# A product-keys stage with its key splits on GpSimd and its thresholds read from PSUM, and a last mixture-of-experts stage without its hardware loop

## The chip, the core and the metric

The kernel runs on one core of one Trainium2 chip. The metric is the device time of the whole kernel in microseconds (us); the time before is the median of three runs. The core's engines are TensorE (PE; its weight loads are listed as PEld), VectorE (DVE), ScalarE (ACT), GpSimd (POOL) and SyncE (SP, which issues most DMAs). A matmul goes to PSUM, which has eight banks of 512 f32 values a partition; GpSimd can't read PSUM.

## What is computed

Eight layers run one after the other over x of 4 x 1024 tokens of 128 values: four attention-like and four feed-forward, each followed by a layernorm of x plus its result. Two feed-forward layers are touched by the change. The first is the product-keys layer (`L2_ffn`):

```python
xn = _rmsnorm(x, norm_w)
q = (xn @ w_q.T).reshape(b, t, H, 2, DK)          # H = 8 heads
sim1 = einsum('bthd,hkd->bthk', q[..., 0, :], keys[:, :, 0, :])   # 32 keys a side
sim2 = einsum('bthd,hkd->bthk', q[..., 1, :], keys[:, :, 1, :])
s1, i1 = top_k(sim1, 8); s2, i2 = top_k(sim2, 8)
all_sc = s1[..., :, None] + s2[..., None, :]
fs, pk = top_k(all_sc, 8)                          # best 8 of 1024 sums a head
hidden = gelu(einsum('btd,bthkd->bthk', xn, expert_down[fi])) * relu(fs)
return einsum('bthk,bthkd->btd', hidden, expert_up[fi])
```

The second is the last layer (`L3_ffn`): a sigmoid gate picks 2 of 8 experts a token; the token times its score goes through that expert (128 -> 176, squared relu, -> 128, in bf16), and a shared expert in f32 is added.

## The kernel before, in words

Each layer is a stage with programs of its own for the engines, which are tied together by semaphores only. A stage works on batches of 1024 tokens (8 tiles of 128 tokens; a half is 4 tiles). Each engine carries out its program in the order in which it is written, so the order of the calls in the loops is the schedule.

**Product keys** (`product_keys_stage`), 32 tiles of 8 heads. The kernel doesn't gather experts. For each tile and head it makes all 1024 sums of the two sides' scores, keeps those that reach the head's eighth best, and adds the kept levels of all heads to one weight for each of the 1024 experts; that times the gelu of all experts goes through `up`.

- `score` (PE) makes a tile's 512 similarities in one bank of the ring A. `take_sims` (ACT, L1965 and L1966) copies them out in f32 and in bf16. `rest_of` (L2055) and `low_of` (L2061), both on DVE, with `take_middle` (ACT, L1971) between them, split each value in three bf16 parts. `transpose_parts` (PE, L2192) turns these in four fills of the ring, and `take_partsT` (ACT, L1977) copies each fill out. All that is done for tile t + 2 while tile t is at work.
- `build_sum` (PE, L2216) makes the 1024 sums of one head in two banks of the ring S (three banks), two heads ahead. `take_sum` (ACT, L1996) copies the two halves to SBUF, where there is room for four heads.
- `keep` (DVE, L2088) compares a head's sums with its least kept value and multiplies: both inputs are the copy in SBUF.
- `add_level` (PE, L2224) adds eight transposes of the level into the two banks of `weights`. After head 7, `weigh` (DVE, L2095) multiplies `weights` by the gelu; the next tile's `add_level` of head 0 has to wait for that, since it starts the two banks anew.
- `project_down` (PE, L2200) and `gelus` (ACT, L1985) make the gelu of a later half, two fills of A a tile, `project_up` (PE, L2235) is the product with `up`; `finish` and `normalise` (DVE, with GpSimd's `rsqrt` between them) end a half.

Ring A is the queue that all of score, gelu product and turned parts go through, in the order of `fills_of_A`. Before, it has two banks: PE may claim a bank once the fill before the last one has been copied out.

```python
to_act = [m.psum(f"to_act{i}", [P, HALF]) for i in range(2)]
sum_banks = [m.psum(f"sum{i}", [P, HALF]) for i in range(3)]
```

**The last stage** (`routed_experts_stage`) runs a hardware loop over the 4 batches. In a pass PE turns x, makes the gates and the shared expert's hidden values, and turns the scores' parts; then 8 units follow (a pair of experts on one half): `widen` (PE, L3022) spreads the scores, `scale` (DVE, L2926) multiplies x by them, `project_up` (PE, L3032 and L3036), relu (ACT, L2899), `square` (DVE, L2933) and `project_down` (PE, L3049), which has the hidden values as weights and is cut in four matmuls of 128 columns. DVE then adds x and normalises the half. `Fori` passes don't overlap: DVE ends a batch (`finish(1)`, `normalise(1)`) before it begins the gates of the next one. GpSimd squares the shared expert's hidden values (L2866).

## Time and profile before

| | |
|---|---|
| median of 3 runs | 2315.13 us (2308.87 to 2318.24) |
| profiled execution, its own time | 2313.05 us |
| its span, first to last instruction | 2311.2 us |
| product-keys stage | about 930 to 1563 us of the span |
| last stage | about 2136 to 2311 us |
| PE, DVE, ACT, POOL busy over the span | 84%, 69%, 52%, 27% |
| TensorE's granted clock, mean | 0.90 of full speed |

A row of the profile gives a line of the kernel, an engine, what is written from what, the count, and then busy time and mean duration, or (in the timeline) start and duration in us; an x4 in the timeline merges four instructions, and the duration is that of all. "[0.86 <-ACT ...]" is idle time of the engine before the row, and what ended it. Matmuls are pipelined: a group's last one runs on while the next group starts. A row of windows gives the stretch, its length, the busy time (and instructions) of PE, PEld, DVE, ACT and POOL in it, then PEclk, the DMA engines' share and GB/s. PEclk is the granted clock as a share of 2.4 GHz; 0.50 is the lower level, 1.2 GHz.

### The profile page before, as it was taken

To read this page: it belongs to the slowest core of one execution; us is meant where nothing else is said; L and a number is where in the kernel's file an instruction comes from. 1 tells how busy PE (TensorE), PEld (TensorE's weight loads), DVE (VectorE), ACT (ScalarE), POOL (GpSimd) and SP (SyncE) were. 2 spreads that over 40 slices of the span, in tenths; PEclk is the share of its full clock that TensorE was granted. 3 is DMA by queue.
4 is the path that set the end of the run, shared out by engine and by line. 5 is a ranking of instruction groups with operands and counts; after the bars stand their busy time and mean duration, and the time that the engine had idled before them with its cause. 6 is when DMAs were issued, how large, how long until landed. Compare 5 with 4: busy or idle time off the path is not lost. (4 is left out here: it accounts for less than half of the span.)

```text
span 2311.2 us, 33205 instructions
## 1 busy us (share of the span) xinstructions
PE 1950.1 (84%) x10882; PEld 1310.8 (57%) x10882; DVE 1595.5 (69%) x3840; ACT 1203.7 (52%) x2540; POOL 630.5 (27%) x774
## 2 busy tenths in 40 slices
PE   8999789996799995799999999987778776775897
PEld 5666544443577773587778777774324333334544
DVE  4555457785278887388898899873368666676676
ACT  3333355652355542588788877850245444554343
POOL 2222147776012122000000000000055555554111
PEclk9999989997899997799999999996688888887877
DMA  2000010000200000000000000005011111111100
GB/s 83 27 27 18 33 66 1 19 10 10 91 10 10 19 10 5 24 1 6 15 6 3 14 6 6 6 1 198 1 36 38 44 48 47 48 45 56 51 27 27
DMA packets 35266, 68.90 MB, mean 30 GB/s; under 512 B 8598, under 2 KB 19935, under 8 KB 34359
## 3 DMA queue, kind: packets, MB, share of 16 engines
q1 hardware_dynamic: 26934, 50.34, 6.3%
q0 software_dynamic: 8192, 16.79, 2.8%
q8 instruction: 77, 1.26, 0.2%
q14 instruction: 63, 0.51, 0.1%
HBM read 54.52 MB, written 12.58 MB: 29 GB/s over the span
## 5 line engine op out<-in xcount | busy, mean ns | idle before, releaser
L2758 PE MATMUL tk_to_act<-tk_keys,tk_xT 128*128 128x512 f32 x512 | 270.3, 672 | 94.9 <-issue 57.9
L1996 ACT ACTIVATE pk_sums<-pk_sum 128x512 f32<-128x512 f32 x512 | 278.8, 601 | 110.2 <-PE pk_sum L2216 107.8
L2088 DVE SCALAR_TENSOR_TENSOR pk_level<-pk_sums,pk_least 128x1024 f32<-128x1024 f32 x256 | 321.5, 1276 | 7.7 <-ACT pk_sums L1996 6.4
L2442 POOL DMA_INDIRECT tk_values<-top_keys_values,tk_index x256 | 243.9, 953 | 299.0 <-DVE tk_index L2607 224.3
L2224 PE MATMUL pk_weights<-product_keys_early_ident,pk_level 128*128 128x128 f32 x2048 | 271.8, 276 | 31.2 <-DVE pk_level L2088 30.1
L2224 PEld LDWEIGHTS pk_weights<-product_keys_early_ident,pk_level 128*128 128x128 f32 x2048 | 225.5, 141 | 65.1 <-DVE pk_level L2088 49.5
L2507 ACT ACTIVATE tk_scores<-tk_to_act 128x512 f32<-128x512 f32 x256 | 143.3, 594 | 209.7 <-PE tk_to_act L2758 112.3
L2758 PEld LDWEIGHTS tk_to_act<-tk_keys,tk_xT 128*128 128x128 f32 x512 | 101.5, 212 | 243.5 <-issue 181.9
L1667 PEld LDWEIGHTS er_outs<-experts_early_w,er_hT 128*128 128x128 f32 x1024 | 134.0, 192 | 59.8 <-issue 56.4
L1102 PE MATMUL ml_outs<-experts_early_we,ml_xT 128*128 128x512 f32 x320 | 162.5, 635 | 3.0 <-DVE ml_r L967 3.0
L2605 DVE MAX8 tk_best<-tk_scores 128x8 f32<-128x4096 f32 x32 | 141.4, 4418 | 32.1 <-issue 16.3
L2216 PE MATMUL pk_sum<-pk_lay_corners,pk_partsT 96*128 96x256 bf16 x1024 | 154.2, 272 | 4.0 <-DVE pk_weighed L2095 3.1
L2607 DVE FIND_INDEX8 tk_index<-tk_best,tk_scores 128x8 uint32<-128x4096 f32 x32 | 141.4, 4419 | 0.0
L223 POOL TENSOR_TENSOR pk_plus_eps<-pk_moments,pk_eps 128x4 f32<-128x4 f32 x8 | 11.9, 1482 | 466.3 <-DVE pk_moments L207 466.3
L1667 PE MATMUL er_outs<-experts_early_w,er_hT 128*128 128x128 f32 x1024 | 134.5, 275 | 0.0
L1369 ACT ACTIVATE er_hT<-er_to_act,experts_early_b 128x512 f32<-128x512 f32 x128 | 85.6, 687 | 93.1 <-PE er_to_act L1656 92.2
L1656 PE MATMUL er_to_act<-er_xT,experts_early_w 128*128 128x512 f32 x256 | 133.4, 603 | 0.0
L1977 ACT ACTIVATE pk_partsT<-pk_to_act 96x1024 bf16<-96x1024 bf16 x128 | 131.6, 1033 | 0.0
L967 DVE SCALAR_TENSOR_TENSOR ml_r<-ml_outs,ml_gates,ml_r 128x128 f32<-128x128 f32 x384 | 103.3, 341 | 19.7 <-PE ml_outs L1102 15.6
L2216 PEld LDWEIGHTS pk_sum<-pk_lay_corners,pk_partsT 96*128 96x128 bf16 x1024 | 99.2, 97 | 29.9 <-DVE pk_weighed L2095 11.1
L854 ACT ACTIVATE ml_scaled<-ml_outs,ml_gates 128x128 f32<-128x128 f32 x256 | 70.2, 390 | 84.0 <-PE ml_outs L1102 84.0
L1102 PEld LDWEIGHTS ml_outs<-experts_early_we,ml_xT 128*128 128x128 f32 x320 | 59.7, 201 | 63.6 <-issue 50.3
(396 smaller groups left out, 3731.5 us busy)
## 6 DMA issues: line engine op xcount, KB each, us to landing
tk_scores<-top_keys_compress SPq DMA_DIRECT2D x1, 4096.0 KB
tk_values<-top_keys_values,tk_index POOLq DMA_INDIRECT x256
att_x_proj<-x_first SPq DMA_DIRECT2D x4, 512.0 KB, 5.2
att_x_res<-x_first SPq DMA_DIRECT2D x4, 512.0 KB
x_after_attention<-att_y SPq DMA_DIRECT2D x4, 512.0 KB
ml_x<-x_after_attention SPq DMA_DIRECT2D x4, 512.0 KB, 3.4
experts_early_w<-experts_w SPq DMA_DIRECT2D x2, 1024.0 KB
x_after_attention<-ml_y SPq DMA_DIRECT2D x8, 256.0 KB, 2.0
```

The source lines that it names most:

```text
L1102: pe.matmul(outs[f % len(outs)][:], xT[:, b % 2, t * P:(t + 1) * P], we[:, n * PER_FILL:(n + 1) * PER_FILL, :].rearrange("p e d -> p (e d) ...
L1656: pe.matmul(bank[:], w1[:, n, :], xT[:, t % 2, :], start=True, stop=True).then_inc(A.full.sem, 1)
L1667: ins = pe.matmul(bank[:, s * P:(s + 1) * P], hT[:, (t * CHUNKS + n) % (LAG + 1), s * P:(s + 1) * P], w2[:, n, :], start=k == 0 and s == 0 ...
L1996: act.activation(sums[:, n % SUMS, half * HALF:(half + 1) * HALF], bank[:], ACT.Copy).then_inc(S.free.sem, 1)
L2088: dve.scalar_tensor_tensor(level[:, n % LEVELS, :], sums[:, n % SUMS, :], least[:, t % 2, h:h + 1], sums[:, n % SUMS, :], ALU.is_ge, ALU.m ...
L2216: ins = pe.matmul(by_column[:, j], partsT[:, t % 3, h * FILLS + c, :], lay_corners[:, c], start=True, stop=True)
L2224: ins = pe.matmul(weights[:, ch * P:(ch + 1) * P], level[:, n % LEVELS, ch * P:(ch + 1) * P], ident[:], is_transpose=True, start=h == 0 an ...
L2442: pool.indirect_dma_start(out=values[:, slot, k, :], out_offset=None, in_=c["values"], in_offset=bass.IndirectOffsetOnAxis(ap=index[slot][ ...
L2507: act.activation(scores[:, t % KEPT, ch * HALF:(ch + 1) * HALF], bank[:], ACT.Copy).then_inc(S.free.sem, 1)
L2605: steps.link(dve.max(best[:, slot, :], scores[:, t % KEPT, :]))
L2607: dve.max_index(index[slot][:], best[:, slot, :], scores[:, t % KEPT, :]).then_inc(index_ready, 1)
L2758: pe.matmul(bank[:], xT[:, b, at * P:(at + 1) * P], keys[:, ch * HALF:(ch + 1) * HALF], start=True, stop=True).then_inc(S.full.sem, 1)
```

## The change

In the product-keys stage: `rest_of` and `low_of` move from DVE to GpSimd, at a tile's start; `sum_banks` become two tiles of two banks each, so that DVE's `keep` reads one of its inputs in PSUM, and `build_sum` of head n + 2 waits until `keep` of head n is done; `take_sum` is one copy of 1024 values; ring A gives up a bank and has one. `keep` of head 0 comes ahead of `weigh` of the tile before. `project_up` is halved between heads 0 and 1, the gelu products and the part transposes follow the level in each head.

```diff
-    SUMS = 4
+    SUMS = 2
-        to_act = [m.psum(f"to_act{i}", [P, HALF]) for i in range(2)]
-        sum_banks = [m.psum(f"sum{i}", [P, HALF]) for i in range(3)]
+        to_act = [m.psum("to_act", [P, HALF])]
+        sum_banks = [m.psum(f"sum{i}", [P, E]) for i in range(SUMS)]
...
+            def rest_of(t):
+                pool.wait_ge(A.free.sem, taken_from_A("sims", t, 0))
+                pool.tensor_tensor(rest[:], sims[:, t % KEPT, 0:SIMS].rearrange("p (c k) -> p c k", k=KEYS),
+                                   parts[:, :, 0, :], ALU.subtract)
+            def low_of(t):
+                pool.wait_ge(middle_ready, t + 1)
+                pool.tensor_tensor(parts[:, :, 2, :], rest[:], parts[:, :, 1, :], ALU.subtract)
...
+            def take_sum(n):
+                act.wait_ge(sum_full, n + 1)
+                act.activation(sums[:, n % SUMS, :], sum_banks[n % SUMS][:], ACT.Copy).then_inc(sum_kept, 1)
...
-                    take_sum(next_built(t * HEADS + h))
+                    if t * HEADS + h + SUMS < UNITS:
+                        take_sum(t * HEADS + h + SUMS)
+                    gelus(beside[h:h + 1])
+                    if chained and h == 1:
+                        take_middle(t + 2)
...
-                dve.scalar_tensor_tensor(level[:, n % LEVELS, :], sums[:, n % SUMS, :], least[:, t % 2, h:h + 1],
+                dve.scalar_tensor_tensor(level[:, n % LEVELS, :], sum_banks[n % SUMS][:], least[:, t % 2, h:h + 1],
                                          sums[:, n % SUMS, :], ALU.is_ge, ALU.mult)
...
                 for h in range(HEADS):
+                    keep(t, h)
                     if h == 0 and t > 0:
                         weigh(t - 1)
-                    keep(t, h)
...
+            def build_sum(n):
                 t, h = divmod(n, HEADS)
                 pe.wait_ge(A.free.sem, taken_from_A("partsT", t, FILLS - 1))
+                after(pe, level_ready, n - SUMS + 1)
...
                     if h == 0:
                         if chained:
                             score(t + 2)
-                        project_down(beside[0:1])
                         after(pe, weighed_ready, t)
-                    build_sum(next_built(t * HEADS + h))
-                    if chained:
-                        if h >= HEADS - FILLS:
-                            transpose_parts(t + 2, h - (HEADS - FILLS))
+                    if t * HEADS + h + SUMS < UNITS:
+                        build_sum(t * HEADS + h + SUMS)
                     add_level(t, h)
-                    if h == 0 and t > 0:
-                        project_up(t - 1)
+                    if h < 2:
+                        if t > 0:
+                            project_up(t - 1, range(h * PER_HALF, (h + 1) * PER_HALF))
+                        project_down(beside[h:h + 1])
+                    if chained and h >= HEADS - FILLS:
+                        transpose_parts(t + 2, h - (HEADS - FILLS))
```

PE where one tile of product keys ends and the next begins (L2192 the parts, L2224 the level, L2182 the score, L2200 a gelu product, L2216 the sums, L2235 the product with up), before:

```order
L2192 MATMUL pk_to_act<-pk_ident_b,pk_parts 96x128 x8
L2224 MATMUL pk_weights<-product_keys_early_ident,pk_level 128x128 x8
L2182 MATMUL pk_to_act<-pk_w_sim,pk_xnT 128x512
L2200 MATMUL pk_to_act<-pk_xnT,product_keys_early_down 128x512
L2216 MATMUL pk_sum<-pk_lay_corners,pk_partsT 128x16x16 x4
L2224 MATMUL pk_weights<-product_keys_early_ident,pk_level 128x128 x8
L2235 MATMUL pk_to_dve<-product_keys_early_up,pk_weighed 128x128 x8
```

and in the change (L2171 the parts, L2161 the score, L2197 the level, L2179 a gelu product, L2189 the sums, L2209 the product with up):

```order
L2197 MATMUL pk_weights<-product_keys_early_ident,pk_level 128x128 x8
L2171 MATMUL pk_to_act<-pk_ident_b,pk_parts 96x128 x8
L2161 MATMUL pk_to_act<-pk_w_sim,pk_xnT 128x512
L2189 MATMUL pk_sum<-pk_lay_corners,pk_partsT 128x16x16 x4
L2197 MATMUL pk_weights<-product_keys_early_ident,pk_level 128x128 x8
L2209 MATMUL pk_to_dve<-product_keys_early_up,pk_weighed 128x128 x4
L2179 MATMUL pk_to_act<-pk_xnT,product_keys_early_down 128x512
```

Two fills of ring A, the last parts and the score, now stand next to each other, where a level stood between them; the gelu product moved behind the level.

ACT over heads 0 to 4 of a tile in the change (L1973 and L1974 the similarities, L1997 the sums, L1993 a gelu, L1979 the middle part, L1985 the turned parts):

```order
L1973 ACTIVATE pk_sims<-pk_to_act 128x512
L1974 ACTIVATE pk_parts<-pk_to_act 128x16x32
L1997 ACTIVATE pk_sums<-pk_sum 128x1024
L1993 ACTIVATE pk_gelu<-pk_to_act 128x512
L1997 ACTIVATE pk_sums<-pk_sum 128x1024
L1993 ACTIVATE pk_gelu<-pk_to_act 128x512
L1979 ACTIVATE pk_parts<-pk_rest 128x16x32
L1997 ACTIVATE pk_sums<-pk_sum 128x1024 x3
L1985 ACTIVATE pk_partsT<-pk_to_act 96x1024
```

The second gelu and the middle part now both stand ahead of the copy of head 4's sums; before, the second gelu came after it.

In the last stage the loop is written out over all 32 units. The next batch's x, gates, shared hidden values and parts are made in units 0 to 5 of the batch before (x in three buffers, the rest in two); a half is finished two units after its last product. `project_down` takes its weights as the stationary side, with one matmul of 512 columns for four of 128; the result is the half turned, so ACT copies it out (`take_out`) and PE turns it back (`turn_out`, four transposes) for DVE. Ring A has two banks instead of three.

```diff
-            with dve.Fori(0, B) as b:
...
+            for unit in range(ALL):
+                b, u = divmod(unit, UNITS)
+                more = b + 1 < B
+                if unit + 1 < ALL:
+                    scale(unit + 1)
+                for k in range(PER_UNIT):
+                    square(unit, k)
+                if u == 2 and b > 0:
+                    finish(b - 1, 1)
+                if u == 3 and b > 0:
+                    normalise(b - 1, 1)
+                if more and u == 3:
+                    score_of(b + 1)
+                if more and u == 4:
+                    parts_of(b + 1)
+                if u == 6:
+                    finish(b, 0)
+                if u == 7:
+                    normalise(b, 0)
...
-                        for i in range(PER_HALF):
-                            last = pair == PAIRS - 1 and k == PER_UNIT - 1 and i == PER_HALF - 1
-                            ins = pe.matmul(out[g][:, i * P:(i + 1) * P], hidden[0:units, n % HIDDEN_SLOTS, i * P:(i + 1) * P],
-                                            w, start=False, stop=last)
+                    ins = pe.matmul(outs[g][:], w, hidden[0:units, n % HIDDEN_SLOTS, :], start=False,
+                                    stop=pair == PAIRS - 1 and k == PER_UNIT - 1)
```

## Rows read from the trace of the kernel before

**Rows 1.** Windows of the product-keys stage and of one of its tiles: busy time by engine

```profile
930.00:1565.00 635.00, 582.48 (x4896) 488.79 (x4896) 534.11 (x1385) 486.74 (x875) 31.95 (x27) 0.98 0.02 8
1003.37:1021.16 17.79, 17.35 (x151) 14.65 (x150) 15.83 (x39) 16.73 (x42) 2.20 (x2) 1.00 0.01 1
```

**Rows 2.** Timeline, product keys, heads 5 to 7 of a tile: start, duration, engine

```profile
1000.52 1.04 PE L2224 MATMUL pk_weights<-product_keys_early_ident,pk_level 128*128 128x128 f32 x8
...
1001.18 1.05 ACT L1977 ACTIVATE pk_partsT<-pk_to_act 96x1024 bf16<-96x1024 bf16 x1
...
1001.40 0.60 PE L2216 MATMUL pk_sum<-pk_lay_corners,pk_partsT 96*128 96x256 bf16 x4
...
1001.84 0.61 PE L2192 MATMUL pk_to_act<-pk_ident_b,pk_parts 128*96 128x128 bf16 x8
1002.08 1.12 ACT L1996 ACTIVATE pk_sums<-pk_sum 128x512 f32<-128x512 f32 x2
...
1002.29 1.04 PE L2224 MATMUL pk_weights<-product_keys_early_ident,pk_level 128*128 128x128 f32 x8
```

**Rows 3.** Timeline, product keys, the start of the next tile

```profile
1003.17 1.02 PE L2182 MATMUL pk_to_act<-pk_w_sim,pk_xnT 128*128 128x512 f32 x2
1003.37 1.23 DVE L2095 TENSOR_TENSOR pk_weighed<-pk_weights,pk_gelu 128x1024 f32<-128x1024 f32 x1 [1.47 <-PE pk_weights L2224]
...
1004.22 0.30 PEld L2200 LDWEIGHTS pk_to_act<-pk_xnT,product_keys_early_down 128*128 128x128 f32 x2 [0.86 <-ACT pk_partsT L1977]
...
1006.77 1.95 PE L2235 MATMUL pk_to_dve<-product_keys_early_up,pk_weighed 128*128 128x128 f32 x16
...
1008.56 0.60 PE L2216 MATMUL pk_sum<-pk_lay_corners,pk_partsT 96*128 96x256 bf16 x4
```

**Rows 4.** Groups by line: the thresholds

```profile
L2088 DVE SCALAR_TENSOR_TENSOR pk_level<-pk_sums,pk_least 128x1024 f32<-128x1024 f32 x256 | 321.5, 1276 | 7.7 <-ACT pk_sums L1996 6.4
```

**Rows 5.** Timeline, VectorE: starts of four of the 32 gelu products

```profile
985.58 1.22 DVE L2095 TENSOR_TENSOR pk_weighed<-pk_weights,pk_gelu 128x1024 f32<-128x1024 f32 x1 [1.47 <-PE pk_weights L2224]
...
1040.39 1.23 DVE L2095 TENSOR_TENSOR pk_weighed<-pk_weights,pk_gelu 128x1024 f32<-128x1024 f32 x1 [1.34 <-PE pk_weights L2224]
...
1060.52 1.22 DVE L2095 TENSOR_TENSOR pk_weighed<-pk_weights,pk_gelu 128x1024 f32<-128x1024 f32 x1 [1.34 <-PE pk_weights L2224]
...
1521.79 1.22 DVE L2095 TENSOR_TENSOR pk_weighed<-pk_weights,pk_gelu 128x1024 f32<-128x1024 f32 x1 [1.48 <-PE pk_weights L2224]
```

**Rows 6.** Timeline, ScalarE: the copy of one gelu fill, first tile

```profile
953.48 0.59 ACT L1985 ACTIVATE pk_gelu<-pk_to_act 128x512 f32<-128x512 f32 x1
```

**Rows 7.** One line of the routed-token stage: a GpSimd tensor_tensor of this size

```profile
L1332 POOL TENSOR_TENSOR er_base<-er_y,er_out_b x8: 1265/1266/1272, 644.3 to 891.4; 128x512 f32<-128x512 f32 x8
```

**Rows 8.** Timeline, last stage: VectorE with and TensorE at half clock

```profile
2163.08 1.08 DVE L2933 TENSOR_TENSOR moe_hidden<-moe_relu 128x512 bf16<-128x512 bf16 x3
...
2165.28 1.08 DVE L2933 TENSOR_TENSOR moe_hidden<-moe_relu 128x512 bf16<-128x512 bf16 x3
...
2203.19 1.03 PE L3022 MATMUL moe_scores_wide<-moe_partsT,moe_lay 24*128 24x512 bf16 x2
...
2207.25 1.03 PE L3022 MATMUL moe_scores_wide<-moe_partsT,moe_lay 24*128 24x512 bf16 x2
```

**Rows 9.** Windows, last stage: half clock, then the three gaps between last finishes

```profile
2196.00:2216.00 20.00, 20.00 (x81) 8.89 (x80) 14.20 (x29) 9.46 (x18) 0.00 (x0) 0.50 0.00 0
2179.88:2222.56 42.68, 39.73 (x216) 21.19 (x216) 31.01 (x83) 17.89 (x32) 6.49 (x8) 0.76 0.11 37
2222.56:2261.25 38.69, 34.99 (x216) 19.00 (x216) 28.17 (x84) 17.55 (x32) 6.53 (x8) 0.87 0.13 41
2261.25:2303.14 41.89, 38.23 (x216) 21.09 (x216) 28.36 (x83) 17.67 (x32) 6.53 (x8) 0.80 0.08 25
```

**Rows 10.** Timeline, last stage: a VectorE subtraction beside a GpSimd square

```profile
2148.63 1.04 POOL L2866 TENSOR_TENSOR moe_s_hidden<-moe_s_relu 128x512 f32<-128x512 f32 x1 [12.46 <-ACT moe_s_relu L2889]
2148.81 0.94 DVE L236 TENSOR_TENSOR moe_rest<-moe_score,moe_parts 128x64 f32<-128x64 f32 x1
```

More of the change, by code:

```diff
@@ new lines, in turn_out @@
+            def turn_out(b, g):
+                half = b * HALVES + g
+                pe.wait_ge(outT_ready, half + 1)
+                after(pe, turned_free, half)
+                for i in range(PER_HALF):
+                    ins = pe.transpose(turned[:, i * P:(i + 1) * P], outT[:, g, i * P:(i + 1) * P], ident[:])
+                ins.then_inc(turned_full, 1)
+            for g in range(HALVES):
+                transpose_x(0, g)
+            gates(0)
+            for n in range(SHARED):
+                shared_hidden(0, n)
```

572 lines of the change are left out of this document (300 added, 272 removed).

## The prediction, made before the changed kernel ran

> **What bounds the kernel now.** The change touches two stages, so I read those and leave the rest of the span alone. I took the windows of each stage first, then one ordinary tile of product keys in the timeline, then the waits, and last the batches of the last stage.
>
> In product keys the row of one tile shows PE busy for 17.35 of 17.79 us at the full clock, DVE 15.83, ACT 16.73 [rows 1]: PE sets the pace. What PE's work amounts to comes from start to next start. A level takes 0.88, a head's sums 0.44, a fill of turned parts 0.45 [rows 2]; the last matmul of a group runs on for 0.16 after that (1.04 against 0.88), so the score and each gelu product, 1.02 long, occupy 0.86, and the product with `up` 1.79 [rows 3]. A tile is 8 x (0.88 + 0.44) + 4 x 0.45 + 3 x 0.86 + 1.79 = 16.7 us. PE therefore waits only about 1.1 us a tile: for the last parts' copy and for `weigh` at the tile's start [rows 3], and once for a threshold. The change leaves PE's matmuls in this stage as they are, so that 1.1 us is all that it can win in an ordinary tile. From the first to the thirtieth gelu product there are 29 tiles in 536.2 us [rows 5]; at 17.79 they would be 515.9, so tiles that end a half or start a batch cost 20.3 more (one gap of 20.13 is in [rows 5]).
>
> In the last stage the three gaps between last `finish`es are 42.68, 38.69 and 41.89 us, mean 41.1, with DVE busy 31.0, 28.2 and 28.4 [rows 9]. At full clock a unit takes 2.20 us and DVE paces it; at the lower clock, 1.2 GHz, it takes 4.06 and PE paces it [rows 8]. In 2196 to 2216 the clock is 0.50 throughout [rows 9]. The other 10 to 13 us of a gap are the drain of one pass and the gates of the next, in which DVE and PE take turns.
>
> **Product keys, part by part.** *Splits to GpSimd.* 64 subtractions leave DVE. On GpSimd I price one at 1.27 us, from a tensor_tensor of the same 128x512 f32 [rows 7]. I cost them at nothing: the first starts when the similarities are copied, the second must be done before PE turns the parts at head 4, four heads later, over 8 us of PE's work, and even three times the price fits. DVE's 1.4 us a tile don't shorten the tile either, as DVE isn't the pace.
>
> *Threshold from PSUM.* Not in the trace in this form; the nearest row from below is DVE's 1024-wide product with one input in PSUM, 1.22 us [rows 3], from above the present threshold, 1.28 [rows 4]. I take 1.28. What counts is the new wait: PE builds the sums of head n + 2 only after the threshold of head n. One turn of that circle is 0.44 + 0.16 for the sums, 0.1 hand-over, 1.03 copy (an ACT copy of 1024 takes 1.05 [rows 2]), 0.05, 1.28, 0.06: 3.1 us for two heads. PE's own work for two heads is 2.64 (heads 2, 3) to 3.54 (4 to 7), so the circle binds where heads are light and is nearly tight elsewhere.
>
> *One bank for ring A.* PE can't write a fill before ACT has emptied the one before. In heads 4 to 7 the parts (0.16 to end, 0.1, copy 1.03, 0.05 = 1.34) are hidden by the next head's sums and level (1.32), with ACT's sum copies between them (0.90 from start to start [rows 2]): I carry 0.1 a tile. At the tile's end nothing stands between the last parts and the next score: PE has no other work and waits the whole **1.33 us**. Before, the same place cost part of the 0.86 of [rows 3], because a second bank was free for the score.
>
> *Head 4.* ACT has, after the second gelu product's last matmul: 0.16 + 0.1, gelu 0.50 (0.59 less the usual overlap [rows 6]), middle part 0.50, copy of head 4's sums 1.03, hand-over 0.05, threshold 1.28, 0.06 = 3.7 us, while PE has two heads, 2.64: **1.05 us** of waiting that the old order didn't have in this size.
>
> *Threshold ahead of `weigh`.* It takes the 0.3 to 0.6 us off that PE waits at a tile's start now, but the wait of 1.33 lies over the same time: `weigh` is done before the score is. So nothing is added for it.
>
> An ordinary tile becomes 16.7 + 1.33 + 0.1 + 1.05 = 19.2 us, 1.4 more; over 29 tiles +41. In tiles that end a half, `finish` now falls into head 4's wait, and only `normalise` shows; by the same walk the extras fall from 20.3 to about 13.5: 7 ends of halves at 0.9, three norms of x at 1.7, three turned x at 0.7: -7.
>
> *First tiles.* 8 gelu fills and 8 of parts now alternate between PE and ACT. A gelu fill is 0.86 + 0.16 + 0.1 + 0.59 + 0.05 = 1.76 against 0.9 to 1.0 now (ACT's pace); a parts fill 0.45 + 1.34 = 1.79 against 0.9. That is 16 x 0.85 and two scores, +15; with PE idle half the time its clock may stay at 1.2 GHz, which makes it up to +30. I take +20. *Last two tiles*: no fills, the threshold ahead of `weigh` helps, -2.
>
> Product keys: +41 - 7 + 20 - 2 = **+52 us**. Ends: +12 (head 4's wait absent, first tiles at +13) and +85 (first tiles +30, 0.8 us more a tile where ACT's order holds up heads 5 to 7).
>
> **Last stage.** What is written out lets a batch's gates run beside the one before: a gap falls from 41.1 to DVE's work. I take 28.4 from the undisturbed gaps [rows 9] plus 1.1 for stalls: 29.5, three times -11.6 = -35. The down projection streams as many columns as before (one matmul of 512 for four of 128), so PE stays at 3.84 of the 4.06 at 1.2 GHz and about 1.9 at 2.4 GHz, below DVE's 2.20. The end is longer by the copy of the turned half (0.6), its turning and two hand-overs: +2. The clock is the open part. It fell here after stretches in which PE waited for DVE at a batch's start, and those go away but for one; I leave three half-clock units, 3 x 1.86: +6. **-27 us**, ends -38 (never slow, no stalls) and -3 (half of the 32 units at 4.06: 16 x 1.86 = 30 back, less 2 of gaps).
>
> A row weighs on it: a subtraction of 64 columns took 0.94 us beside a GpSimd square of two SBUF inputs, until that ended [rows 10]; such squares now run in the middle of units. The Trainium skill's "SBUF — State Buffer", section "Who interferes with whom", says that a DVE instruction with two SBUF inputs and a GpSimd instruction that reads SBUF exclude each other, and one with a single SBUF input doesn't; the trace agrees on the first half. By it the new threshold would run freely beside GpSimd's splits, where the old form, held up twice a tile, would have cost DVE up to 2.5 us.
>
> **Sum.** +52 - 27 = +25. Against the profiled execution (2313.05, span 2311.2) that is 2338; the median shown is 2.1 higher, so I give **2340 us**.
>
> **Rivals.**
> *Product keys nearly as fast as before* (ends faster): the head 4 wait vanishes because ACT reaches the fifth sums in time, the waits that remain are 1.33 a tile (18.05 us, +7 over 29), the first tiles cost 13, and the last stage wins 33. +12 - 33 = -21: **2294**. It decides at the ordinary tile: at 20 - 2 - 7 + 29 d = 27 the two stages cancel, d = 0.55, a tile of 18.3 us. For it: ACT is busy 16.73 of 17.79, but loses 0.06 a head with one copy for two, and DVE loses 1.4 us. Against: the order of ACT's program. Chance 0.25.
> *The gains and losses cancel*: waits as walked, but first tiles at the full clock and the last stage at its best, or a tile of 18.3: **2315**. Chance 0.13.
> *Last stage mostly at 1.2 GHz*: PE paces it, -3: **2364**. For it: 20 us on end at 0.50 with PE never idle [rows 9]. Chance 0.09.
> *Product keys lose the clock*: with 2.5 us of waiting a tile PE falls to 1.2 GHz for a part. A tile's 16.7 us of PE become 33.4, 14 more than 19.2; five tiles are +70: **2410**. Now the tile runs at 1.00 throughout [rows 1]. Chance 0.08. The Trainium skill's "TensorE: Matmul & The Clock Gate", Part 4, holds that transposes don't count as activity for the clock. The row speaks against it: 96 of the tile's 151 matmuls are transposes, at clock 1.00; by the page the stage should have run at the lower level already.
>
> **How the numbers follow.** The forecast has 0.45, with a range of its own of 2327 to 2362. No change means within 0.5% (11.6 us, 2303.5 to 2326.7), about what a measurement of this kernel can tell. Faster 0.25 is the first rival, same 0.13 the second, slower 0.45 + 0.09 + 0.08 = 0.62. The range 2290 to 2375 leaves out the clock rival (0.08) and the far part of the first (0.1).
>
> **What would show it.** In the changed trace: PE idle 1.3 us before each score, released by the copy of the parts; PE waiting about 1 us for a threshold before head 4; gaps between gelu products of 19.2; DVE's threshold at 1.2 to 1.3 us; the first threshold about 20 us later; last finishes 29 to 32 us apart. A gap below 18.3, or a score that starts at once, makes the prediction wrong.

## The result, and the profile after the change

| | before | after |
|---|---|---|
| median of this comparison | 2312.72 us (4 runs) | 2352.91 us (4 runs, 2343.39 to 2353.88) |
| ratio, 95% interval | 1 | 1.016 (1.0128 to 1.0198) |
| profiled execution, its span | 2311.2 us | 2350.2 us |
| first to last gelu product (32 tiles) | 568.5 us | 607.9 us |
| ordinary tile of product keys | 17.79 us | 19.35 us |
| first gelu product at | 985.6 us | 1009.6 us |
| top keys, not touched: last store of product keys to last `y` | 568.1 us | 575.5 us |
| last stage: from there to the end | 181.1 us | 149.3 us |

The kernel got slower by 1.6%. Product keys end 63.4 us later, the last stage is 31.8 us shorter, and the 7.4 us between them lie in a stage that nobody changed. Nine other profiles put that stage at 562 to 585 us with no pattern (three more at 465 to 470, see below), so they are its scatter.

Windows of product keys in the changed kernel, the stage and one tile (columns as in [rows 1]):

```profile
930.00:1628.00 698.00, 589.97 (x4879) 488.23 (x4879) 501.27 (x1321) 468.55 (x617) 92.37 (x88) 0.95 0.02 6
1131.95:1151.27 19.32, 17.25 (x150) 14.56 (x150) 14.65 (x38) 13.98 (x17) 2.25 (x2) 1.00 0.01 2
```

PE is busy 17.25 us, against 17.35 in [rows 1], but the tile is 1.5 longer. DVE has 1.2 us less to do. ACT's 16.73 in [rows 1] is not that of an ordinary tile: eight squares of the next batch are in it, and tiles without them have 14.7, so ACT has 0.7 less. Neither shortens anything. The timeline shows where PE stands still. At a tile's end, then at the light heads of the same tile:

```profile
1130.12 0.62 PE L2171 MATMUL pk_to_act<-pk_ident_b,pk_parts 128*96 128x128 bf16 x8
...
1130.78 1.03 ACT L1985 ACTIVATE pk_partsT<-pk_to_act 96x1024 bf16<-96x1024 bf16 x1
...
1131.95 1.10 PE L2161 MATMUL pk_to_act<-pk_w_sim,pk_xnT 128*128 128x512 f32 x2 [1.21 <-ACT pk_partsT L1985]
...
1139.22 0.60 ACT L1993 ACTIVATE pk_gelu<-pk_to_act 128x512 f32<-128x512 f32 x1 [1.56 <-PE pk_to_act L2179]
...
1139.71 0.62 ACT L1979 ACTIVATE pk_parts<-pk_rest 128x512 bf16<-128x512 f32 x1
1140.23 1.93 ACT L1997 ACTIVATE pk_sums<-pk_sum 128x1024 f32<-128x1024 f32 x2
...
1140.77 1.04 PE L2197 MATMUL pk_weights<-product_keys_early_ident,pk_level 128*128 128x128 f32 x8
1141.28 2.48 DVE L2075 SCALAR_TENSOR_TENSOR pk_level<-pk_sum,pk_least,pk_sums 128x1024 f32<-128x1024 f32 x2 [1.51 <-ACT pk_sums L1997]
1142.71 0.60 PE L2189 MATMUL pk_sum<-pk_lay_corners,pk_partsT 96*128 96x256 bf16 x4 [0.90 <-DVE pk_level L2075]
```

Read it from start to start. The last parts' matmuls begin at 1130.12 and would be followed 0.45 us later; the score begins at 1131.95, so 1.38 us are lost, and ACT's copy of those parts fills them. The level of 1140.77 would be followed at 1141.65, and the sums begin at 1142.71: 1.06 lost. With 0.15 for the parts and 0.07 behind the score that is 2.66 on PE's 16.7, which gives 19.36.

The groups by line say the same for the whole stage: the threshold takes 1278 ns against 1276 in [rows 4], but DVE is idle 158 us ahead of it where it was 7.7, and PE waits for it at the sums:

```profile
L2075 DVE SCALAR_TENSOR_TENSOR pk_level<-pk_sum,pk_least,pk_sums 128x1024 f32<-128x1024 f32 x256 | 324.6, 1278 | 158.3 <-ACT pk_sums L1997 157.8
...
L2189 PE MATMUL pk_sum<-pk_lay_corners,pk_partsT 96*128 96x256 bf16 x1024 | 154.9, 273 | 41.0 <-DVE pk_level L2075 38.6
```

The gelu products on DVE, first, thirtieth and last:

```profile
1009.63 1.22 DVE L2082 TENSOR_TENSOR pk_weighed<-pk_weights,pk_gelu 128x1024 f32<-128x1024 f32 x1
...
1587.77 1.22 DVE L2082 TENSOR_TENSOR pk_weighed<-pk_weights,pk_gelu 128x1024 f32<-128x1024 f32 x1
...
1617.52 1.22 DVE L2082 TENSOR_TENSOR pk_weighed<-pk_weights,pk_gelu 128x1024 f32<-128x1024 f32 x1 [1.19 <-PE pk_weights L2197]
```

From first to thirtieth 578.1 us, 41.9 more than in [rows 5]; from there to the last 29.7 against 32.3. The first is 24.1 late, but that is not the whole price of the start, since in this pair the stage also began 4.4 us earlier in the changed kernel. Its first matmuls, before and then changed:

```profile
930.65 13.81 PE L2163 MATMUL pk_to_dve<-product_keys_early_keys,product_keys_early_wq 128*128 128x16 f32 x64 [8.31 <-PEq L154]
```

```profile
926.22 13.81 PE L2142 MATMUL pk_to_dve<-product_keys_early_keys,product_keys_early_wq 128*128 128x16 f32 x64 [8.24 <-PEq L154]
```

From there the first gelu product took 54.9 us before and 83.4 after: 28.5 more. In the stage's first tiles the windows read, for before and then for the changed kernel:

```profile
964.00:972.00 8.00, 5.93 (x57) 4.33 (x57) 5.47 (x23) 7.81 (x13) 0.00 (x0) 1.00 0.01 3
```

```profile
964.00:972.00 8.00, 4.17 (x18) 2.25 (x18) 0.00 (x0) 3.29 (x5) 0.00 (x0) 0.50 0.00 0
```

The clock column is the point. Before, the clock was at its upper level from about 950; after, it stays at 0.50, which is 1.2 GHz, until 996, and one gelu fill then takes 2.82 us:

```profile
954.56 2.04 PE L2179 MATMUL pk_to_act<-pk_xnT,product_keys_early_down 128*128 128x512 f32 x2 [0.78 <-ACT pk_gelu L1993]
957.38 2.05 PE L2179 MATMUL pk_to_act<-pk_xnT,product_keys_early_down 128*128 128x512 f32 x2 [0.78 <-ACT pk_gelu L1993]
```

In the last stage, the windows up to and between the four `finish`es of second halves (as [rows 9]; the last batch has no next one beside it):

```profile
2235.23:2265.63 30.40, 29.92 (x132) 12.28 (x133) 25.99 (x73) 19.25 (x35) 5.53 (x6) 1.00 0.03 9
2265.63:2296.03 30.40, 29.66 (x127) 12.03 (x130) 29.42 (x84) 18.82 (x34) 7.02 (x8) 1.00 0.11 36
2296.03:2325.87 29.84, 28.58 (x116) 10.72 (x118) 29.31 (x85) 17.64 (x32) 7.03 (x8) 1.00 0.05 18
2325.87:2342.76 16.89, 14.70 (x58) 5.47 (x58) 15.72 (x51) 9.36 (x17) 2.56 (x4) 1.00 0.04 16
```

The first line is only the stretch of the same length ahead of the first of them; the gaps are the other lines, 30.4, 29.8 and 16.9 where [rows 9] had 41.1 on average. So the three gaps together are 46.1 us shorter, while the first batch, which now has the second one's preparation beside it and is finished later, takes 14.9 longer from the stage's start to its `finish`. In the gap of 30.40 DVE is busy for 29.42 and PE for 29.66, so these rows don't tell which of the two sets the pace. The clock stays at 1.00.

### The profile page after: what moved, and what is told of

Same layout as the page of the kernel before. It is cut to its first block and busy times, and to the rows that moved or that the text cites. A ratio compares the mean times of both kernels' runs of the same rounds, so it can differ in the third digit from the quotient of the medians.

```text
span 2350.2 us, 31320 instructions
## 1 busy us (share of the span) xinstructions
PE 1935.5 (82%) x10521; PEld 1277.3 (54%) x10530; DVE 1562.8 (66%) x3776; ACT 1191.0 (51%) x2292; POOL 690.5 (29%) x838
## 5 line engine op out<-in xcount | busy, mean ns | idle before, releaser
L2075 DVE SCALAR_TENSOR_TENSOR pk_level<-pk_sum,pk_least,pk_sums 128x1024 f32<-128x1024 f32 x256 | 324.6, 1278 | 158.3 <-ACT pk_sums L1997 157.8
L1997 ACT ACTIVATE pk_sums<-pk_sum 128x1024 f32<-128x1024 f32 x256 | 258.8, 1021 | 54.0 <-PE pk_sum L2189 53.8
L2197 PE MATMUL pk_weights<-product_keys_early_ident,pk_level 128*128 128x128 f32 x2048 | 266.5, 273 | 0.5 <-DVE pk_level L2075 0.5
L2197 PEld LDWEIGHTS pk_weights<-product_keys_early_ident,pk_level 128*128 128x128 f32 x2048 | 232.3, 141 | 4.1 <-DVE pk_level L2075 0.9
L2189 PE MATMUL pk_sum<-pk_lay_corners,pk_partsT 96*128 96x256 bf16 x1024 | 154.9, 273 | 41.0 <-DVE pk_level L2075 38.6
L1923 POOL TENSOR_TENSOR pk_rest<-pk_sims,pk_parts 128x512 f32<-128x512 f32 x32 | 36.0, 1124 | 406.0 <-ACT pk_parts L1974 406.0
L2189 PEld LDWEIGHTS pk_sum<-pk_lay_corners,pk_partsT 96*128 96x128 bf16 x1024 | 92.3, 97 | 109.0 <-issue 98.8
L1985 ACT ACTIVATE pk_partsT<-pk_to_act 96x1024 bf16<-96x1024 bf16 x128 | 130.9, 1022 | 22.5 <-PE pk_to_act L2171 22.5
L967 DVE SCALAR_TENSOR_TENSOR ml_r<-ml_outs,ml_gates,ml_r 128x128 f32<-128x128 f32 x384 | 103.3, 340 | 16.9 <-PE ml_outs L1102 15.1
```

The lines of the kernel that those rows point to most:

```text
L1997: act.activation(sums[:, n % SUMS, :], sum_banks[n % SUMS][:], ACT.Copy).then_inc(sum_kept, 1)
L2075: dve.scalar_tensor_tensor(level[:, n % LEVELS, :], sum_banks[n % SUMS][:], least[:, t % 2, h:h + 1], sums[:, n % SUMS, :], ALU.is_ge, ALU ...
L2189: ins = pe.matmul(by_corner[:, i, j], partsT[:, t % 3, h * FILLS + c, :], lay_corners[:, c], start=True, stop=True)
L2197: ins = pe.matmul(weights[:, ch * P:(ch + 1) * P], level[:, n % LEVELS, ch * P:(ch + 1) * P], ident[:], is_transpose=True, start=h == 0 an ...
```

## The experiments

The runs form four groups, each with its own runs of before: medians of 2311.4, 2319.8, 2202.8 and 2317.1 us. In the third group the untouched top-keys stage took 465 to 470 us, some 100 less than in all others, so totals compare only within a group, and across groups I compare stages. The totals (median, number of runs, and the median of before in the same group) and the stage lengths of all profiles, in us:

| run | total / before | ordinary tile | first gelu product | from the stage's first matmul | first to last | last stage |
| --- | --- | --- | --- | --- | --- | --- |
| before | 2312.7 (4) | 17.79 | 985.6 | 54.9 | 568.5 | 181.1 |
| after | 2352.9 (4) / 2312.7 | 19.35 | 1009.6 | 83.4 | 607.9 | 149.3 |
| e1_last_stage | 2293.8 (4) / 2311.4 | 17.79 | 986.6 | 55.0 | 568.5 | 156.1 |
| e2_product_keys | 2382.0 (4) / 2311.4 | 19.35 | 1010.1 | 83.4 | 607.9 | 174.1 |
| e3_one_bank | 2419.0 (1) / 2311.4 | 20.1 | 1016.5 | 84.8 | 647.5 | 174.3 |
| e4_banks_back | 2289.9 (4) / 2311.4 | 17.80 | 986.6 | 54.8 | 564.5 | 156.5 |
| e7_middle_later | 2347.1 (1) / 2319.8 | 18.85 | 1014.1 | 83.4 | 602.5 | 151.2 |
| e8_score_later | 2371.1 (1) / 2319.8 | 19.53 | 1014.5 | 86.5 | 615.7 | 149.2 |
| e9_spread | 2317.2 (1) / 2319.8 | 18.77 | 1011.4 | 85.8 | 584.4 | 149.2 |
| e10_prep_serial | 2363.2 (1) / 2319.8 | 19.35 | 1014.2 | 83.4 | 607.9 | 158.7 |
| e11_one_bank_new_order | 2243.1 (1) / 2202.8 | 19.16 | 1009.8 | 84.2 | 601.4 | 151.6 |
| e12_best | 2171.5 (4) / 2202.8 | 17.65 | 982.0 | 55.4 | 560.5 | 151.3 |
| e13_best_dve_splits | 2217.3 (5) / 2202.8 | 18.8 to 20.4 | 982.3 | 55.3 | 602.6 | 151.0 |
| e14_middle_ahead | 2258.9 (6) / 2317.1 | 16.87 | 981.9 | 54.8 | 540.7 | 149.0 |

**Each stage alone.** The edits are whole functions: `routed_experts_stage` of the change in the kernel before, and `product_keys_stage` of the change in the kernel before.

> Product keys of before, last stage of the change. If the two stages are independent, this is before less what the last stage gained in the traces (180.8 us from the last store of top keys to the end before, 149.0 after, 31.8): 2281 us, product keys at 17.79 us a tile as before. Rival: the last stage gained only because it came later or after a differently loaded product-keys stage, or part of the 31.8 is scatter of that stage's clock: then 2290 to 2300, with slow units at clock 0.50 in the last stage.

> Product keys of the change, last stage of before. Product keys' last store came 63.4 us later in the changed kernel: 2376 us, if this is the stage's own cost. Top keys, which the change doesn't touch, took 568.1 us before and 575.5 after (last store to last store); rival: these 7 us belong to the change (what it leaves in flight at the stage's end), then this run shows 575 again, otherwise anything between 568 and 576 is the stage's own scatter.

Measured: 0.990 of before (0.984 to 0.996) and 1.033 (1.028 to 1.038). The tile lengths are those of before and after to 0.02 us, so neither stage changes the other's pace. Product keys alone cost 3.3%, more than the whole change, and the last stage gives part of it back. The total of the first run, 2293.8 us, is not the 2281 that I expected but lies in the range of the rival: part of the 31.8 us is scatter of that stage. The last stage of before scatters as well, 174.1 us in the second run against 181.1, so its gain is 18 to 32 us over these profiles. Top keys took 574.4 and 564.9 us, so its 7 us did not follow the product keys. In the first run the last stage was 156.1 and not 149.3, and the windows show units at the lower clock:

```profile
2168.00:2176.00 8.00, 7.74 (x25) 3.89 (x23) 4.45 (x10) 3.95 (x7) 0.00 (x0) 0.50 0.00 0
2176.00:2184.00 8.00, 8.00 (x23) 4.04 (x23) 3.29 (x8) 1.90 (x4) 0.00 (x0) 0.56 0.01 3
```

The units of the first batch ran at 1.2 GHz for some 20 us here and in e4_banks_back, and not in the changed kernel.

**One bank alone.**

```
-        to_act = [m.psum(f"to_act{i}", [P, HALF]) for i in range(2)]
+        to_act = [m.psum("to_act", [P, HALF])]
```

> Before, with one bank in ring A in place of two, all else as it was, last stage too. If the single bank is what costs the stage's start, the first gelu product comes at 1005 to 1012 us as in the changed kernel (1009.6), against 985.6. A tile has then the wait before the score (about 1.3 us, of which before already had 0.5), and, as in this order the first gelu product follows the score at once, a second one for the copies of the similarities (about 1.3): 19.2 to 20.2 us a tile, product keys 60 to 95 us longer, 2375 to 2405. Rival, the bank costs little and the loss is the new head order and the threshold's circle: a tile stays below 18.3 and the first gelu product below 995.

Measured: 2419.0 us in one run, a tile of 20.1, the first gelu product at 1016.5, product keys 110 us longer. The tile is inside what I gave, the start 4 us, product keys 15 and the total 14 us above it. The second wait is there, behind the score:

```profile
1107.56 1.10 PE L2182 MATMUL pk_to_act<-pk_w_sim,pk_xnT 128*128 128x512 f32 x2 [0.69 <-ACT pk_partsT L1977]
1108.70 0.60 ACT L1965 ACTIVATE pk_sims<-pk_to_act 128x512 f32<-128x512 f32 x1 [1.28 <-PE pk_to_act L2182]
1109.93 1.10 PE L2200 MATMUL pk_to_act<-pk_xnT,product_keys_early_down 128*128 128x512 f32 x2 [1.27 <-ACT pk_parts L1966]
```

So with the old order one bank is dearer than in the change, whose order puts the sums and a level behind the score.

**The banks back.** The changed kernel, with two banks in ring A, three of 512 for the sums and four copies of sums in SBUF:

```
-    SUMS = 2
+    SUMS = 4
+    AHEAD = 2
...
-        to_act = [m.psum("to_act", [P, HALF])]
-        sum_banks = [m.psum(f"sum{i}", [P, E]) for i in range(SUMS)]
+        to_act = [m.psum(f"to_act{i}", [P, HALF]) for i in range(2)]
+        sum_banks = [m.psum(f"sum{i}", [P, HALF]) for i in range(3)]
...
-                dve.scalar_tensor_tensor(level[:, n % LEVELS, :], sum_banks[n % SUMS][:], least[:, t % 2, h:h + 1],
+                dve.scalar_tensor_tensor(level[:, n % LEVELS, :], sums[:, n % SUMS, :], least[:, t % 2, h:h + 1],
```

> The changed kernel with the banks of before: two in ring A, three of 512 for the sums, sums built two heads ahead, and so the threshold from two SBUF copies; the new order, the splits on GpSimd and the new last stage stay. My theory (one bank and the two-deep circle are the loss; order and splits cost nothing): a tile at 16.9 to 17.6 us, the first gelu product at 985, product keys 10 to 25 us below before, 2260 to 2275 in all. Rival 1, GpSimd's splits hold up the threshold with two SBUF inputs: thresholds of 2 us and more beside L1923 and L1929, a tile above 18.5, 2300 or more. Rival 2, the new order itself (second gelu product ahead of the middle part, level before the turned parts) is the loss: a tile of 18.5 to 19.3.

Measured: 0.990 of before (0.985 to 0.995). The start is back at 986.6 and the tile at 17.80: the whole loss goes with the banks, and both rivals fall. But the tile didn't go below 17.79, and the total of 2289.9 us is above the 2260 to 2275 that I expected. PE loses 0.44 us at the tile's start, where it asks for `weigh` before it builds sums that don't need it, and 0.34 and 0.29 at heads 3 and 4, where ACT is late:

```profile
1098.90 0.61 PE L2198 MATMUL pk_sum<-pk_lay_corners,pk_partsT 96*128 96x256 bf16 x4 [0.23 <-DVE pk_weighed L2087]
...
1105.25 0.60 ACT L1995 ACTIVATE pk_gelu<-pk_to_act 128x512 f32<-128x512 f32 x1 [1.49 <-PE pk_to_act L2184]
...
1105.74 0.62 ACT L1981 ACTIVATE pk_parts<-pk_rest 128x512 bf16<-128x512 f32 x1
1106.26 2.05 ACT L2002 ACTIVATE pk_sums<-pk_sum 128x512 f32<-128x512 f32 x4
1106.36 0.38 PE L2198 MATMUL pk_sum<-pk_lay_corners,pk_partsT 96*128 96x256 bf16 x2
...
1106.91 0.39 PE L2198 MATMUL pk_sum<-pk_lay_corners,pk_partsT 96*128 96x256 bf16 x2 [0.16 <-ACT pk_sums L2002]
```

**Bank and circle apart.** The kernel of the last run with one bank in ring A (the edit of e3_one_bank).

> The kernel with the banks of before (17.80 us a tile, first gelu product at 986.6), with one change: ring A has one bank, the other bank lies unused. This parts the two things that the banks back undid together. By my steps the single bank brings the 1.38 us before the score, less the 0.44 that PE there already waited for weigh, and all of the first tiles: a tile at 18.6 to 18.9, the first gelu product at 1009 to 1014. Then the two-deep circle is worth the other 0.5 to 0.8 of 19.35. Rival, the circle is the larger part: a tile of 18.0 to 18.3 here.

Measured: a tile of 19.16 and the first gelu product at 1009.8. The single bank is 1.36 of the 1.55 us a tile and all of the start. The rest of the bank layout (the two-deep circle, and with it the threshold from PSUM and the single copy of 1024) adds only 0.19. The 1.36 is a net figure: 1.44 us before the score and some 0.35 around the parts and behind the score, less the 0.44 for `weigh`, which the bank's wait now covers. My expectation was 0.3 too low: the 0.62 at heads 3 and 4 stays, and each fill of parts waits 0.05 to 0.1.

**The two waits of the changed tile.** On ACT the middle part behind the fifth head's sums:

```
-                    if chained and h == 1:
+                    if chained and h == 2:
                         take_middle(t + 2)
```

> The changed kernel with the middle part's copy moved on ACT from ahead of the fifth head's sums to behind them. My step for head 4 (gelu 0.5, middle 0.5, sums 1.03, threshold 1.28 against two heads of PE): PE's wait before head 4 falls by 0.5 us, a tile from 19.37 to 18.9, product keys 13 to 15 us shorter, the waits before the score unchanged. Rival, the wait comes from the two-deep circle alone and only moves: a tile stays at 19.2 to 19.4.

Measured: a tile of 18.85, as the step says. But first to last is only 5.4 us shorter, not 13 to 15: the four tiles that only end a half grew from 20.91 to 21.6 and 22.42, and the three that also turn the next batch's x stayed at 22.06. Perhaps `finish`, which the wait at head 4 had hidden, came into the open; no run shows it.

The score behind the first level:

```
                     if h == 0:
-                        if chained:
-                            score(t + 2)
                         after(pe, weighed_ready, t)
...
                     add_level(t, h)
+                    if h == 0 and chained:
+                        score(t + 2)
```

> The changed kernel with the score moved on PE from the tile's start to behind the first head's sums and level (and on ACT the similarities behind that head's sums). My step for ring A (1.33 us of waiting before each score, because nothing stands between the last parts and it): that wait is covered and goes; what comes in its place is 0.5 us for weigh, which the wait covered, and 0.3 to 0.6 for the gelu product that now waits for the copies of the similarities: a tile at 18.9 to 19.2, 19.37 in the changed kernel. Rival, PE's time at the tile's start is set by DVE (threshold, weigh) and not by the bank: a tile stays at 19.3 or grows.

Measured: 19.53, the rival's result. The wait for the bank is gone, and these two stand in its place:

```profile
1138.21 0.61 PE L2189 MATMUL pk_sum<-pk_lay_corners,pk_partsT 96*128 96x256 bf16 x4 [0.83 <-DVE pk_weighed L2082]
...
1141.83 1.10 PE L2179 MATMUL pk_to_act<-pk_xnT,product_keys_early_down 128*128 128x512 f32 x2 [0.38 <-ACT pk_parts L1974]
```

From start to start 1.0 and 0.55 us. I had taken the first at 0.5, as if the sums of 0.44 could run beside `weigh`; but PE asks for `weigh` ahead of them.

Both, and the gelu products one head later:

```
                     if h < 2:
                         if t > 0:
                             project_up(t - 1, range(h * PER_HALF, (h + 1) * PER_HALF))
-                        project_down(beside[h:h + 1])
+                    if h in (1, 2):
+                        project_down(beside[h - 1:h])
```

> The changed kernel with both moves, and with the two gelu products behind the levels of heads 1 and 2 in place of 0 and 1. By my steps the score's wait is covered, the gelu products no longer wait for the similarities, and the fifth head's sums come ahead of the second gelu: 16.7 of work, 0.5 for weigh, 0.1 for the parts, up to 0.5 at one of the heads 4 or 5: 17.8 to 18.2 us a tile, product keys 30 to 45 us shorter than in the changed kernel, the first gelu product still at 1009. Rival, the two-deep circle (3.1 us for two heads, 2.64 of PE) holds up each light head and sets the tile: 18.8 or more.

Measured: 18.77, first to last 23.5 us shorter than in the change. Between my two figures, nearer the rival's: `weigh` 1.0, and the circle 0.6 and 0.4 at heads 5 and 6:

```profile
1140.35 0.60 PE L2190 MATMUL pk_sum<-pk_lay_corners,pk_partsT 96*128 96x256 bf16 x4 [0.43 <-DVE pk_level L2076]
...
1142.55 0.60 PE L2190 MATMUL pk_sum<-pk_lay_corners,pk_partsT 96*128 96x256 bf16 x4 [0.28 <-DVE pk_level L2076]
```

No order tried brings the change's banks to the tile of before.

**The last stage without its overlap.** The next batch's preparation in one piece, on PE:

```
+                if more and u == 7:
+                    for g in range(HALVES):
+                        transpose_x(b + 1, g)
+                    gates(b + 1)
+                    for n in range(SHARED):
+                        shared_hidden(b + 1, n)
+                    transpose_parts(b + 1)
                 if unit + 1 < ALL:
                     widen(unit + 1)
```

and the same on ACT and DVE.

> The changed kernel; in its last stage the next batch's turned x, gates, shared hidden units and parts are all made ahead of the eighth unit, in one piece, where the change spreads them over units 0 to 5. The orientation of the down projection, the copies and the third x buffer stay. If the overlap is the gain, the gap of last finishes goes back from 30.0 to 40 to 43 us, the stage costs 30 to 38 more, and the clock falls below 1.00 after a batch's start as it did before: 2385 in all. Rival, the gain is the down projection in one matmul of 512 columns for four of 128 and the clock that it keeps: gaps of 32 to 35.

Measured: gaps of 33.8 and 33.9, the stage 158.7 us against 149.3, the rival's range. PE and DVE do take turns again where the next batch starts, but for a short while:

```profile
2257.37 0.60 PE L3079 MATMUL moe_scores_wide<-moe_partsT,moe_lay 24*128 24x512 bf16 x2 [1.10 <-ACT moe_partsT L2906]
...
2257.89 1.29 DVE L2978 TENSOR_TENSOR moe_scaled<-moe_scores_wide,moe_xT 128x512 bf16<-128x512 f32 x2 [2.56 <-PE moe_scores_wide L3079]
```

Without the spreading the stage is 9 us longer, where the change as a whole took 25 to 32 us off at a steady upper clock. The first part of the expectation holds for the clock alone: it fell to 0.50 in both gaps and once ahead of them, for 3.4 us each time (2250.6 to 2254.0 is the first), so the 9 us hold the price of that too. The rest lies in what this run kept: units that still run across the border of a batch, outputs finished two units later, the down projection in its new orientation, the clock. I didn't part those.

**A version that beats both.** From e4_banks_back, with its own waits edited. First the wait for `weigh` behind the sums and the middle part at head 2; then the same with both splits on DVE:

```
                     if h == 0:
                         if chained:
                             score(t + 2)
-                        after(pe, weighed_ready, t)
                     if t * HEADS + h + AHEAD < UNITS:
                         build_sum(t * HEADS + h + AHEAD)
+                    if h == 0:
+                        after(pe, weighed_ready, t)
```

> The kernel with the banks of before, with the two waits edited that its timeline still shows: PE asks for weigh behind the sums of the tile's first head in place of ahead of them (0.44 us), and ACT copies the middle part behind the sums of the fifth head (0.34 and 0.29 at heads 3 and 4). 17.80 less up to 1.05: a tile at 16.8 to 17.1, extras of ends of halves 0.3 to 1.0 larger because finish comes into the open, product keys 15 to 28 us shorter, 2255 to 2270 in all. Rival, PE isn't the pace any more below 17.8 (DVE 15.27 or ACT 13.1 to 16.7 busy in a tile, or the threshold's chain): a tile stays at 17.5 or more.

> The same as the run before it, with both splits back on DVE (rest behind the threshold of head 1, low behind that of head 3). If the splits on GpSimd are worth nothing, as I costed them, this is the same time within 3 us and a tile within 0.1. DVE is busy 15.27 in a tile of 17.80 without them, 16.6 with them. Rival, at a tile of 16.9 DVE with the splits becomes the pace or delays single thresholds: 0.3 to 0.8 us a tile, 8 to 25 us longer.

Measured: 0.986 of before (0.983 to 0.988) with a tile of 17.65, the rival's; and 1.007 (1.005 to 1.010) with tiles of 18.8 to 20.4. In the first, GpSimd's low part now ran beside thresholds that read two SBUF inputs, and both got longer. The low part begins inside one threshold and takes 0.6 us more than alone, the next threshold begins inside the low part and takes 0.6 more:

```profile
1083.87 1.28 DVE L2080 SCALAR_TENSOR_TENSOR pk_level<-pk_sums,pk_least 128x1024 f32<-128x1024 f32 x1 [0.99 <-ACT pk_sums L2002]
...
1084.43 1.74 POOL L1931 TENSOR_TENSOR pk_parts<-pk_rest,pk_parts 128x512 bf16<-128x512 f32 x1 [5.86 <-ACT pk_parts L1981]
...
1085.36 1.90 DVE L2080 SCALAR_TENSOR_TENSOR pk_level<-pk_sums,pk_least 128x1024 f32<-128x1024 f32 x1 [0.21 <-ACT pk_sums L2002]
```

In the second I had expected the same time within 3 us; it was 46 us longer, beyond the rival's 8 to 25 too. DVE's low part waits for the middle part and holds the thresholds behind it:

```profile
1406.42 0.69 DVE L2047 TENSOR_TENSOR pk_parts<-pk_rest,pk_parts 128x512 bf16<-128x512 f32 x1 [2.20 <-ACT pk_parts L1963]
```

That comes from where ACT makes the middle part here, so the run doesn't tell what the splits on DVE cost in a better order; that wasn't tried.

Last, the middle part ahead of the second gelu, in the 1.49 us that ACT waits for PE there:

```
+                    if chained and h == 1:
+                        take_middle(t + 2)
                     gelus(beside[h:h + 1])
-                    if chained and h == 1:
-                        take_middle(t + 2)
```

> The kernel with the banks of before, PE's wait for weigh behind the first sums, and ACT's middle part ahead of the second gelu, where ACT waits 1.49 us for PE, in place of behind it or behind the fifth sums. If PE's waits at heads 3 and 4 come from ACT being late, they go without GpSimd's low part falling beside two thresholds: a tile at 16.8 to 17.3 (17.65 with the middle part behind the fifth sums, 17.80 with it behind the gelu), thresholds at 1.28 but for one a tile of up to 1.9, product keys 15 to 25 us shorter than before, and with the last stage 0.975 to 0.982 of before. Rival, DVE's order (threshold, pairs and best in heads 3 to 5) sets the pace: a tile at 17.4 to 17.7, ratio 0.985 to 0.99.

Measured: **0.974 of before (0.970 to 0.978)**, 2258.9 us beside 2317.1. The tile is 16.87 us, and PE is busy in every part of it:

```profile
1084.00:1101.00 17.00, 17.00 (x154) 14.71 (x152) 15.63 (x38) 14.59 (x26) 2.84 (x2) 1.00 0.01 1
```

First to last is 27.8 us shorter than before. This is PE's 16.7 us of work, nearly bare. The thresholds took 1.43 us at most, but the low part still falls beside them (median 1.75 us). The two moves gave this together; the wait for `weigh` wasn't moved alone.

## Why the prediction was right, step by step

**PE sets the pace and its matmuls stay.** Right: 17.25 busy in the tile, and 16.87 from start to start once the waits were edited away. ACT's 16.73 was no ordinary tile's (14.7), but only the case for the first rival used it.

**One bank, 1.33 at the score.** Right: 1.38, released by the copy of the parts. e11_one_bank_new_order gives the bank 1.36 a tile by itself, but as a sum of other terms, so that these two agree is chance.

**Head 4, 1.05.** The size was right (1.06), the reason only in part. I put it down to ACT's order meeting the two-deep circle. e4_banks_back has 0.63 at heads 3 and 4 with sums four deep, and undoing the circle, with the threshold from PSUM that goes with it (e11_one_bank_new_order), brings a tile from 19.35 to 19.16 only.

**`weigh`'s place costs nothing.** Right here, since the bank's wait lies over it. e8_score_later shows the 1.0 us that it hides.

**An ordinary tile 19.2, 29 tiles +41.** Measured 19.35 and +45. **Extras from 20.3 to 13.5**: they fell to 17, so -3 and not -7. Ends of halves cost 1.5 us more than an ordinary tile, and 2.7 with the next batch's x turned in them, where I gave 0.9 and 1.6. That `finish` hides in head 4's wait fits the first kind in e7_middle_later, which grew by 0.7 to 1.5 as the wait shrank, and not the second, which stayed. Together +41.9 against +34. **First tiles +20**: +28.5 counted from the stage's first matmul; the +24.1 on the clock of the whole kernel is nearer only because the stage happened to begin 4.4 us earlier. I had 15 for the full clock and 30 for half clock. The clock did stay at 1.2 GHz for the whole fill, and the 30 was the right price: a gelu fill took 2.82 us where I had 1.76 at the full clock, a parts fill 2.26 where I had 1.79. The step that was mis-sized is the +20 that I took between the two. **Last tiles -2**: -2.5. Product keys: +67.8 from their own start (+63.4 with the earlier start) against +52, inside its ends.

**Threshold from PSUM, 1.28.** Measured 1278 ns. **Splits at nothing**: right in the change, where GpSimd ends its low part at about 1141.6 and PE turns the first parts at 1144.02. The rule from the Trainium skill's "SBUF — State Buffer", "Who interferes with whom", can be checked in both forms: with sums read from PSUM, in the changed kernel, no threshold and no low part is held up, though 60 thresholds ran beside a split; with both inputs in SBUF, in e12_best, they are:

```profile
L2075 DVE SCALAR_TENSOR_TENSOR pk_level<-pk_sum,pk_least,pk_sums x256: 1247/1283/1286, 993.8 to 1615.1; 128x1024 f32<-128x1024 f32 x128
...
L1929 POOL TENSOR_TENSOR pk_parts<-pk_rest,pk_parts x32: 1152/1162/1167, 952.2 to 1577.7; 128x512 bf16<-128x512 f32 x32
```

```profile
L2080 DVE SCALAR_TENSOR_TENSOR pk_level<-pk_sums,pk_least x256: 1252/1280/2111, 965.9 to 1540.0; 128x1024 f32<-128x1024 f32 x128
...
L1931 POOL TENSOR_TENSOR pk_parts<-pk_rest,pk_parts x32: 1154/1745/1961, 949.6 to 1506.4; 128x512 bf16<-128x512 f32 x32
```

The columns are least, median and greatest in ns. So the trace agrees with the rule, and the new form does what it should; it just isn't worth two banks here. The 2.5 us a tile that I gave as the most the old form could lose beside GpSimd were far too much: in e4_banks_back, which has that form beside the splits, no threshold took more than 1.44 us and the tile stayed at 17.80. There GpSimd did the waiting (its low part took up to 2.16). In e12_best the 80 thresholds beside a split lost some 13 us together, 0.4 a tile.

**Last stage -27.** Measured -31.8 in this pair, 174 to 181 against 149 to 156.5 over all runs with the same code. Two gaps were 30.1 on average against 29.5. But I had walked three such gaps: the third is 16.9, and the first batch is 14.9 longer, which I had put at nothing. These two nearly cancel (-46.1 + 14.9 = -31.2 where I had -35), and that is luck. I gave the clock 6 us, and from the first unit on it never fell in the changed kernel; it did in e1_last_stage, where 7 us came of it. What I took for the main cause, gates beside the batch before, e10_prep_serial puts at 9 us. One or two 64-column instructions of a batch's gates are still long beside GpSimd's squares, as in [rows 10] (0.95 and 0.93 us in the third batch, where 0.2 is usual), no more than before.

**The sum.** +25 predicted, +39 in the profiles: -4.4 ahead of product keys, +67.8, +7.4 for top keys and -31.8. The first and third are scatter. So product keys were under-priced by 16 us, and the last stage's larger gain and the earlier start gave part of that back. The rival that product keys stay nearly as fast failed at its own point, a tile of 18.3. The rival that they lose the clock holds only for the first tiles: from 1004 on it was 1.00, with 2.7 us of waiting a tile.

## What to carry to other kernels

A ring of one bank cost its reader's whole copy wherever the writer had nothing else in between; ask for every fill what stands ahead of it. At this stage's start there is nothing: with one bank the time from the first score to the first sums was 45.9 us in all eight profiles, at the lower clock, and with two it was 19.1 to 19.7 in all six. A wait often covers others: before you remove one, write down what is late next, since in three of the runs here the next one took the place at once. And when an engine is fully used in all but a microsecond a tile, look for operations of the helpers that can be done while they wait (here one copy on ACT, moved one place forward, and one semaphore wait, moved behind work that doesn't need it): that gave 0.9 us a tile. Freeing DVE of 1.0 us a tile (e4_banks_back) had left it at 17.80; whether the 16.87 needs the splits on GpSimd wasn't tried.

## What the runs showed of the hardware that I had not expected

The granted clock differs between executions of the same code. In the units of its first batch the new last stage stayed near 0.50 for some 20 us in e1_last_stage and e4_banks_back (0.57 over 2160 to 2184 in the first, with PE busy for 23.15 of the 24 us) and ran at 1.00 in the change; the stage was 7 us longer for it. In e7_middle_later the clock fell twice for 3.4 us (2229.8 to 2233.2 and 2260.5 to 2263.9), and the stage was 2 us longer. What PE did ahead of it was the same program, and I found no row that tells them apart.

The untouched top-keys stage took 562 to 585 us in the profiles of three groups and 465 to 470 in the other. Its GpSimd gathers were as long in both (953 ns), so the difference lies in waits. Over 1600 to 2000 us TensorE's clock was 0.81 to 0.90 in e14_middle_ahead and 0.81 to 1.00 in e12_best, DVE was busy for 254 against 335 us, and PE stood still for 64 us ahead of one line's matmuls with no releaser that the profile shows, where e12_best had none of that; the cause stays open.

A threshold with two SBUF inputs and a GpSimd subtraction that overlap don't only delay DVE: GpSimd's went from 1.16 to 1.74 us as well.
